# Value projections as seven block products ahead of the head loop, and one operation for the last score sum and its maximum

## The reference

```python
h_q = (x @ w_q.T).reshape(b, lq, H, DH)
h_k = (key_value_states @ w_k.T).reshape(b, lk, H, DH)
h_v = (key_value_states @ w_v.T).reshape(b, lk, H, DH)
score = jnp.einsum('bqhd,bkhd->bhqk', h_q, h_k)
score = score + position_bias[None]
score = jnp.where(m, score, -jnp.inf)
score = jax.nn.softmax(score, axis=-1)
score = jnp.where(m, score, 0.0)
attn = jnp.einsum('bhqk,bkhd->bqhd', score, h_v).reshape(b, lq, H * DH)
out = attn @ w_out.T
return hidden_states + out
```

## Time and profile before

| what | us |
|---|---|
| median of 3 runs | 1042.22 (1042.18 to 1042.51) |
| the profiled execution's own time | 1042.18 |
| its span, first to last instruction | 1040.4 |
| PE busy in the span | 1011.1 (97%) |
| DVE, ACT, POOL busy | 718.3, 505.4, 463.1 |
| matmuls | 5856 |

### The profile page before, as it was taken

One profiled execution on the slowest core, in us unless ns is written; L12 is line 12 of the kernel. 1 busy time (PEld: TensorE's weight loads), 2 busy tenths in 40 slices (PEclk: granted clock), 3 DMA queues, 4 the chain that ended last, 5 costly groups with the idle time before them and its releaser, 6 DMA issues.

```text
span 1040.4 us, 17490 instructions
## 1 busy us (share of the span) xinstructions
PE 1011.1 (97%) x5856; PEld 885.6 (85%) x5856; DVE 718.3 (69%) x1310; ACT 505.4 (49%) x1223; POOL 463.1 (45%) x402
## 2 busy tenths in 40 slices
PE   8999999999999999999999999999999999799995
PEld 7887888888899998989899998989999897578784
DVE  6768767577767777676777777676767767663615
ACT  7745444555545545455454554554545545343251
POOL 0345775454535435255353453544535434352204
PEclk9999999999999999999999999999999999899997
DMA  7533544422121120211212112212022130300011
GB/s 263 185 140 125 180 163 152 172 94 94 27 93 63 43 93 25 93 63 55 81 35 83 63 55 81 65 54 89 30 89 67 43 114 22 112 20 1 1 41 41
DMA packets 39140, 86.07 MB, mean 83 GB/s; under 512 B 5184, under 2 KB 9280, under 8 KB 39104
## 3 DMA queue, kind: packets, MB, share of 16 engines
q1 hardware_dynamic: 39104, 85.62, 24.4%
HBM read 66.73 MB, written 18.87 MB: 82 GB/s over the span
## 4 chain that ended last, share of the span: by engine, by line
PE 87%; DVE 5%; POOL 3%; ACT 2%; issue 2%; DMA 1%; SPq 0%; DVEq 0%; POOLq 0%; ACTq 0%
PE psum L1656 25%; PE psum L1658 24%; PE psum L1657 24%; PE psum L1662 8%; PE psum L1663 3%; PE psum L1826 3%; DMA raw<-in_dft 1%; POOL cx_lo L768 1%; ACT smx L1026 1%; POOL mix L614 0%; POOL stat L760 0%; POOL stat L758 0%; DVE xn_lo L1226 0%; DVE rsum L1565 0%; DVE acc L1507 0%
## 5 line engine op out<-in xcount | busy, mean ns | idle before, releaser
L614 POOL TENSOR_TENSOR mix<-kf,mix 128x512 fp32r<-128x512 f32 x64 | 113.8, 1778 | 144.6 <-ACT mix L824 144.6
L665 POOL TENSOR_TENSOR smx<-far,bias 128x512 f32<-128x512 f32 x64 | 83.1, 1299 | 173.0 <-DVE smx L1318 172.3
L1656 PE MATMUL psum<-wvq_lo,cx_hi 128*128 128x256 f32 x512 | 149.6, 292 | 0.0
L1658 PE MATMUL psum<-wvq_hi,cx_hi 128*128 128x256 f32 x512 | 144.9, 283 | 0.0
L1657 PE MATMUL psum<-wvq_hi,cx_lo 128*128 128x256 f32 x512 | 144.8, 283 | 0.0
L1026 ACT ACTIVATE smx<-smx,nmax 128x128 f32<-128x128 f32 x256 | 99.7, 390 | 82.8 <-DVE nmax L1324 82.8
L824 ACT ACTIVATE av_hi<-psum 128x512 fp32r<-128x512 f32 x140 | 83.8, 599 | 105.5 <-PE psum L1663 66.7
L1656 PE MATMUL psum<-mix,av_hi 128*128 128x512 f32 x256 | 105.9, 414 | 1.0 <-issue 1.0
L1656 PE MATMUL psum<-xn_lo,wvq_hi 128*128 128x512 f32 x272 | 106.1, 390 | 0.0
L1657 PE MATMUL psum<-xn_hi,wvq_lo 128*128 128x512 f32 x272 | 105.9, 389 | 0.0
L1658 PE MATMUL psum<-xn_hi,wvq_hi 128*128 128x512 f32 x272 | 105.9, 389 | 0.0
(11 more groups left out here) (222 smaller groups left out, 2634.7 us busy)
## 6 DMA issues: line engine op xcount, KB each, us to landing
kf<-k_blocks SPq DMA_DIRECT2D x64, 256.0 KB, 2.6
raw<-in_wk SPq DMA_DIRECT2D x16, 512.0 KB, 3.6
k_blocks<-far SPq DMA_DIRECT2D x32, 256.0 KB, 2.3
raw<-in_wv SPq DMA_DIRECT2D x16, 512.0 KB, 4.9
raw<-in_wq SPq DMA_DIRECT2D x16, 512.0 KB, 3.5
raw<-in_wo SPq DMA_DIRECT2D x16, 512.0 KB, 3.4
raw<-in_ffn SPq DMA_DIRECT2D x10, 512.0 KB, 3.8
k_blocks<-rest SPq DMA_DIRECT2D x16, 256.0 KB, 2.0
```

Source lines behind the costliest of these rows:

```text
L614: g.tensor_tensor(dst_lo, src, dst_hi, ALU.subtract).then_inc(s_lo, 1)
L665: nc.gpsimd.tensor_tensor(bm, far[:, HB * hf:HB * hf + HB, :], g_, ALU.add).then_inc(s_bm_ready, 1)
L1656: mm(out, lhs(0), rhs(1), start=first, stop=False)
L1658: return mm(out, lhs(0), rhs(0), start=False, stop=last)
```

## The change

The values leave the loop. Behind the key pairs come 16 more groups (p = 16 to 31), two for each quad of heads, in which the values of all heads are made by the same seven block products. The context rows or their sums are the stationary operand and the sums of value weights the moving one, 256 columns wide: `product` has 2 * 2 * 3 matmuls for a block, 84 for a group. The blocks are stored to DRAM (`v_blocks`), and each step loads one, whose high part is made by ACT (`v_hi`) and low part by POOL (`v_lo`) from SBUF; before, both came out of PSUM, the low part by DVE. DVE's last sum and maximum of the scores become four `tensor_tensor_reduce`, one per sequence, each 128 wide. Exponentials and probabilities are made in place in two buffers that alternate. PE's order in step n is `project(n+2)`, `turn_probs(n)`, `outputs(n-3)`, `attend(n)`, `scores(n+2)`: queries and scores one step further ahead, outputs one step later. ACT, DVE and POOL are put in a matching order. The query weights move to the buffer `ext`. The feed-forward weights UP are loaded and split during the first and the last pair, all low parts by POOL.

```diff
+V0_PIECE = K0_PIECE + PAIRS
+QUADS = PAIRS // 2
+GROUPS = PAIRS + 2 * QUADS
+K_SETS = PAIRS - 1
...
-        scores_sb, exps, probs, bm = (smx[:, i] for i in range(4))
+        soft, bm = (smx[:, 0], smx[:, 1]), smx[:, 3]
...
+        wq = [ext[i].rearrange("p a n -> p (a n)").rearrange("p (h c n) -> p h c n", h=2, c=DC) for i in (0, 1)]
...
+        psQ, psT = banks[0], banks[2]
+        psO = [banks[1], banks[3]]
...
+        def weights_of(i, w, block):
+            if not is_v(w):
+                return mix[:, 2 * PIECE * i + 2 * P * block:2 * PIECE * i + 2 * P * (block + 1)]
+            if i == 0:
+                return wvq[block // 4][:, HALF * (block % 4):HALF * (block % 4 + 1)].rearrange("p (c n) -> p c n", c=2)
+            return mix[:, :].rearrange("p (c n) -> p c n", c=2)[:, :, 2 * P * block:2 * P * (block + 1)]
+        def set_of(p):
+            return p - 1 if p < PAIRS else K_SETS + (p - PAIRS) // 2
+        def next_set(p):
+            if p < PAIRS:
+                return p
+            return set_of(p) + 1 if p % 2 and p + 1 < GROUPS else None
...
+                if p < PAIRS:
+                    dst = kd[4 * p + i]
+                else:
+                    pair = p - PAIRS - p % 2 + (i in (C21, C22))
+                    dst = vd[4 * pair + 2 * (i in (C12, C22)) + p % 2]
+                sp.dma_start(dst, staged(p, i)).then_inc(s_kst[i], 16)
...
+            def load_v(g, j):
+                if is_first(g):
+                    sp.wait_ge(s_kp_mm, BLOCKS * (GROUPS - 2) + 4)
+                    sp.wait_ge(s_kst[C11 if j < 2 else C12], 16 * (PAIRS + 2))
+                else:
+                    sp.wait_ge(s_v_lo, 4 * g + (j - 3))
+                    for i in range(4):
+                        sp.wait_ge(s_kst[i], 16 * GROUPS)
+                sp.dma_start(vf_row(j), row(vd, 4 * g + j)).then_inc(s_vf[j], 16)
...
                 for i in (C22, C11, C21, C12) if p else range(4):
                     store_block(p, i)
                 if p + SLOTS < PAIRS:
                     load(k_piece(p + SLOTS), t["wk"][p + SLOTS])
+                elif p < PAIRS:
+                    load(V0_PIECE + p + SLOTS - PAIRS, t["wv"][p + SLOTS - PAIRS])
+                elif p % 2 == 0 and p + SLOTS < GROUPS:
+                    for pair in (p + SLOTS - PAIRS, p + SLOTS + 1 - PAIRS):
+                        load(V0_PIECE + pair, t["wv"][pair])
+                elif p == GROUPS - 4:
                     load_wq(0)
+                if p == PAIRS:
+                    for j in range(4):
+                        load_k(0, j)
+            store_block(GROUPS - 1, C22)
+            store_block(GROUPS - 1, C11)
             for j in range(4):
+                load_v(0, j)
+            store_block(GROUPS - 1, C21)
...
+            def group_pool(p):
+                w = next_set(p)
+                if w is not None:
+                    if p < PAIRS:
+                        first_sums(w)
+                    if not is_v(w):
+                        second_sum(w)
+                    weights_lo(w, A11)
+                elif p % 2 == 0:
+                    first_sums(set_of(p) + 1)
                 if p in (3, 6):
                     factors(p // 3 - 1)
                 if p in (6, 8, 10, 12):
                     weighted_row(p - 6)
                     weighted_row(p - 5)
+                if w is not None:
+                    if is_v(w):
+                        second_sum(w)
+                    weights_lo(w, A12)
+                    last_sum(w)
+                    weights_lo(w, A22)
                 if p in (2, 5):
                     shifted_rows(p // 3)
...
+            def v_lo(n, j):
+                split_lo(s_v_hi, s_v_lo, n + 1, vf_row(j).rearrange("p (b n) -> p b n", b=2),
+                         vv[0][:, 2 * j:2 * j + 2, :], vv[1][:, 2 * j:2 * j + 2, :])
+            first_sums(0)
+            second_sum(0)
+            weights_lo(0, A11)
+            weights_lo(0, A12)
+            last_sum(0)
+            weights_lo(0, A22)
+            for p in range(1, GROUPS - 2):
+                group_pool(p)
             wq_lo(0, 0)
             wq_lo(0, 1)
+            k_lo(0, 0)
             bias_and_mask(0, 0, 0)
+            v_lo(0, 0)
+            v_lo(1, 1)
+            k_lo(1, 1)
+            bias_and_mask(1, 0, 1)
             def pair_pool(g):
                 last = is_last(g)
                 for j in range(4):
                     n = 4 * g + j
+                    if not (last and j >= 2):
+                        g2, j2 = after(g, j, 2)
+                        k_lo(n + 2, j2)
+                        v_lo(n + 2, j2)
+                        bias_and_mask(n + 2, g2, j2)
                     if j == 1 and not last:
                         wq_lo(g + 1, 0)
                     if j == 2:
                         if not last:
                             wq_lo(g + 1, 1)
+                        wo_lo(g)
+                    if (is_first(g) or last) and j in (1, 3):
+                        split_low(UP[j // 2 + (2 if last else 0)])
...
+                act.wait_ge(s_q_mm, n + 1)
+                if due(n):
+                    act.wait_ge(s_scores_mm, n)
+                else:
+                    act.wait_ge(s_kp_mm, BLOCKS * (GROUPS - 1))
+                copy_hi(qk[0][:, 0], bank[:, :]).then_inc(s_q_hi, 1)
+            def v_hi(n, g, j):
+                act.wait_ge(s_vf[j], 16 * (g + 1))
+                copy_hi(vv[0][:, 2 * j:2 * j + 2, :], vf_row(j).rearrange("p (b n) -> p b n", b=2)).then_inc(s_v_hi, 1)
...
                 if due(n):
                     act.wait_ge(s_probs_ready, n)
                 for b in range(HB):
+                    a.activation(soft[parity][:, b, :], soft[parity][:, b, :], ACT.Exp, bias=nmax[:, 1, b:b + 1],
                                  accum_out=esum[:, 0, b:b + 1]).then_inc(s_exp_done, 1)
             for p in range(DFT_PIECES):
             t_hi(1)
             k0_copy(C11)
             for block in (A11, S2, S3, S1):
+                weights_hi(0, block)
             k0_copy(C21)
...
             def pair_act(g):
                 last = is_last(g)
                 for j in range(4):
                     n = 4 * g + j
+                    if not (is_first(g) and j == 0):
+                        attended_hi(n - 1, 8 * g - 4 + (4 if j == 3 else -4 if j == 0 else 0) + (0 if j else 4), prev(j))
+                    if not (last and j >= 2):
+                        k_hi(n + 2, *after(g, j, 2))
+                        if due(n - j % 2):
+                            act.wait_ge(s_a_mm, n - j % 2)
+                        v_hi(n + 2, *after(g, j, 2))
                     if j == 1 and not last:
                         act.wait_ge(s_q_mm, 4 * g + 3)
                         wq_hi(g + 1, 0)
                     if j == 2 and not last:
                         act.wait_ge(s_q_mm, 4 * g + 4)
                         wq_hi(g + 1, 1)
+                    if not (last and j >= 2):
+                        q_hi(n + 2, psQ)
+                    if due(n):
+                        act.wait_ge(s_a_mm, n)
+                    hi_of(s_t_mm, s_t_hi, n + 1, flat(pt[0]), psT[:, :])
+                    if not (last and j == 3):
+                        exps_of(n + 1, (j + 1) % 2)
+                    if j == 2:
+                        if due(8 * g):
+                            act.wait_ge(s_o_mm, 8 * g)
+                        wo_hi(g)
+                    if (is_first(g) or last) and j < 2:
+                        ffn_hi(UP[j + (2 if last else 0)])
+                    if last and j == 3:
+                        attended_hi(n, 8 * g, j)
             every_pair(act, pair_act)
...
+            def softmax_in(n, parity):
+                s = soft[parity]
                 dve.wait_ge(s_scores_mm, n + 1)
                 dve.wait_ge(s_bm_ready, n + 1)
                 if due(4 * n):
                     dve.wait_ge(s_exp_done, 4 * n)
-                v.tensor_tensor(scores_sb, psS[:, :, 0], bm, ALU.add).then_inc(s_scores_sum, 1)
+                if due(n - 1):
+                    dve.wait_ge(s_t_mm, n - 1)
+                v.tensor_tensor(s, psS[:, :, 0], bm, ALU.add).then_inc(s_scores_sum, 1)
                 dve.wait_ge(s_scores_sum, n + 1)
-                v.tensor_tensor(scores_sb, psS[:, :, 1], scores_sb, ALU.add).then_inc(s_scores_full, 1)
-                dve.wait_ge(s_scores_full, n + 1)
-                v.tensor_reduce(nmax[:, 0, :], scores_sb, AX.X, ALU.max).then_inc(s_scores_max, 1)
-                dve.wait_ge(s_scores_max, n + 1)
+            def softmax_max(n, parity):
+                s = soft[parity]
+                for b in range(HB):
+                    v.tensor_tensor_reduce(s[:, b, :], psS[:, b, 1], s[:, b, :], 1.0, -3.0e38, ALU.add, ALU.max,
+                                           nmax[:, 0, b:b + 1]).then_inc(s_scores_full, 1)
+                dve.wait_ge(s_scores_full, 4 * n + 4)
```

(129 more changed lines are left out.)

463 lines of the change are left out of this document (180 added, 283 removed).

## The result

The changed kernel takes 1126.39 us (median, 1122.21 to 1130.78), the kernel before 1042.29: ratio 1.0807, 95% interval 1.0766 to 1.0848. It is 84 us slower; 1023 was forecast, between 1015 and 1037. The profiled execution took 1130.78 us, its span is 1129.0.

A forecast was written before the change was run, and what follows sets the result against it. The prediction took PE's list of matmuls to bound the kernel. Its terms summed as 1042.2 - 23.5 (values) + 7.0 (start) - 5.0 (end) + 2.5 (clock) = 1023.2 us, range 1015 to 1037.

The forecast's parts named there:

- the loop's order: Loop, engines' queue order within a step: every wait has 0.9 us or more of cover, so nothing is charged.
- the slower rival: Loop: DVE becomes the bound through costly fused operations; step 8.45 us, time 1063 us; chance 0.10.
- signs of being wrong: DVE without idle time and a loop step above 7.9 us; PE waits inside value groups; loop below full clock.
- the step's arithmetic: Loop, PE's matmuls per step: 10.66 us falls to 7.79, removing 183.7 us over 64 steps.
- Values: Loop and new groups on PE: 183.7 us removed, 1344 matmuls at 0.119 add 160.2, net -23.5 us.
- Rival (3): Value groups don't run at PE's pace: each 10 us group stretched by 1 us, 1039 us; chance 0.03.
- The fused operation: Loop, DVE: each of four 128-column operations costs c = 0.30 us, between 0.13 and 0.48; DVE stays below 7.79.
- rival (1): Loop: DVE becomes the bound, deciding from c = 0.53; at 0.69 the time is 1063 us; chance 0.10.
- Start: Start of the loop: PE waits 9.7 us against some 2.7 before, +7.0 us, between +4 and +9.
- Rival (2): Loop's start costs more, clock included, or POOL's slower price stops the new groups: 1029 to 1037 us; chance 0.15.
- End: End of the loop, last scores to first feed-forward matmul: 26.0 us against 27.1; term -5, between -8 and 0.
- Clock: Half clock behind PE's holes at the loop's start and end: 0 to +5 us, +2.5 taken.

The follow-up runs named there:

- the start moved: Kernel without ACT's wait, with POOL making the low part of keys 1 before those of values 0 and 1 ahead of the loop: 1030.33 us.
- the first hole away: Kernel without ACT's wait, with the last pair's output weights in the query weights' buffer so ACT makes their high part earlier: 1027.48 us.
- the old form: Kernel without ACT's wait, with the last score sum and the maximum as in the kernel before (one 512-wide operation each): 1035.13 us.
- the wait and the old form: Changed kernel, ACT's wait kept, with the last score sum and maximum as in the kernel before: 1151.78 us, ratio 1.1045.

## Why the prediction was wrong

The step that failed is the one on the loop's order: "Every wait has 0.9 us or more of cover, so I charge the loop nothing." In its place the runs showed a hole of 3.85 us and half clock behind it in the first step of 15 pairs, 96 us in all, and without ACT's wait 1031.78. I followed PE's and DVE's waits through a step and took the chain from transposes to low part (1.66 us) out of the trace of before. But that chain starts with an ACT copy, and what stood ahead of it in ACT's queue had changed: the copy of the attended block of the step before, with its wait. The wait's count is a line of the diff, and setting j = 0 in it, to see which output it asks for and when PE makes that one, would have shown it. No rival contained it; the slower rival blamed DVE. What I named as signs of being wrong, a step above 7.9 and less than full clock, did appear, with DVE idle. Where ACT doesn't wait, the step's arithmetic holds: 7.8 us, with 1.2 us of cover.

The other steps, read from the kernel without the wait:
- Values: 5664 matmuls; PE busy throughout the groups, starts 0.120 apart against the 0.119 used, so 1344 take 161.3 and not 160.2; steps 7.80 against 7.79. Right, 1.8 us too low in all. Ahead of them one thing was not in the sum: where the key groups end, PE waits 1.11 and 0.17 us in place of 0.51 before, and the first value matmul starts 1.0 us later (204.45 against 203.41). Rival (3) did not occur.
- The fused operation: c is 0.21, between the bounds of 0.13 and 0.48 and below the 0.30 taken. DVE never becomes the bound: rival (1) fell. That DVE is busy 7.0 us of a step, though 5.69 + 4 x 0.21 is 6.5, comes from the negation of the maximum, 0.79 us here against 0.29 before.
- Start: 9.7 us of waits forecast, 10.5 read in five holes (2.83, 0.64, 2.68, 1.47, 2.92). The holes were right in place, but for the 0.64, and about right in sum; single ones missed by up to 1.2 us, which cancelled. After two of them the clock halved (0.50 over 383 to 387): attend, scores and the first two query matmuls take 4.3 and 4.0 us against the 2.4 of step 1, 3.4 us that the start's term didn't hold. Rival (2) put such a start at 1029 to 1037.
- End: from the last scores to the feed-forward 26.0 forecast, 32.2 found (27.1 before), so 6.2 too low. The hole behind `wo_lo` came as described, 2.67 for 3. What was mis-sized is the clock behind it, and behind the next hole of 1.51 (0.50 over 886 to 892): I counted one spell of half clock, "a shorter hole replaces the one that already pays", and this execution has two. With the start moved, the same end has only the first, a shorter one, and takes 30.0. With the first hole away the stretch takes 26.5; that this is near 26.0 is luck, since the 26.0 held that hole.
- Clock: 2.5 was taken for the whole kernel, and this is the term that was too small even without ACT's wait. Together: 1023 without the loop's holes became 1031.8, inside the range and above the 1017 to 1029 given to the forecast, for these terms. In the profiled execution, the longest of the four and 12.0 us above 1023.2, they sum to 1.8 + 1.0 + (0.8 + 3.4) + 6.2 - 2.5 = 10.7 (values, the hand-over from the keys, start, end, the clock term that is now inside them); 1.3 stay unassigned. The three other runs were 2.7 to 4.5 us shorter, and no trace shows where.

## What to carry to other kernels

When a step moves to another place in an engine's in-order queue, set the loop index into every wait that moves with it, and ask in which step the awaited work is made and what now stands behind the waiting instruction. A hole in PE's work can be paid a second time in the clock behind it: holes of 3.85 us were, in all 15 pairs, holes of 2.5 us in three of 15. So price a hole with the matmuls that follow, as a range, and look at more than one trace. Where the profile names who ended a wait, look for a second end within some hundredths of a microsecond, and for the queue that both came out of.

## What the runs showed of the hardware

The fused operation of 128 columns is two instructions, 0.28 us and a readout of 0.08, and the next one starts 0.21 us after it:

```profile
571.02 0.28 DVE L1433 CUSTOM_DVE_ANT_0 smx<-psum,smx 128x128 f32<-128x128 f32 x1
571.22 0.08 DVE L1433 DVE_READ_ACCUMULATOR2_ANT nmax<- 128x1 f32 x1
571.22 0.28 DVE L1433 CUSTOM_DVE_ANT_0 smx<-psum,smx 128x128 f32<-128x128 f32 x1
...
571.97 0.23 DVE L1436 TENSOR_SCALAR nmax<-nmax 128x4 f32<-128x4 f32 x1
```

The Trainium skill ("VectorE: DVE Perf Modes", "Two Vector instructions with no wait between them") says that an operation which also writes out its accumulator is two instructions, and the trace agrees. But the readout lies under its neighbours here, so four take 0.95 us from the first's start to the next operation's, less than the 1.38 to 1.43 of the pair that they replace.

The same DVE operation of four columns took 0.23 us in one step and 0.97 in another, and in the steps compared it ended 0.02 to 0.03 us behind an operation of POOL. In the kernel without the wait:

```profile
601.71 0.80 DVE L1436 TENSOR_SCALAR nmax<-nmax 128x4 f32<-128x4 f32 x1
...
601.20 1.29 POOL L693 TENSOR_TENSOR av_lo<-wvq_hi,av_hi 128x512 fp32r<-128x512 f32 x1
```

DVE ends at 602.51, POOL at 602.49; with the old form it is 602.84 and 602.81, with the wait and the old form 581.70 and 581.68. So in the loop without the wait a faster sum and maximum mostly lets this operation start its wait earlier. The Trainium skill ("SBUF — State Buffer", "Who interferes with whom") says that a `tensor_scalar` of VectorE that runs in a two-port mode and an operation of GpSimd take a shared pair of ports in turn, each for the whole instruction. The rows agree with that; that this operation ran in such a mode no row shows, and no run changed it to prove the cause.
